# Logits out of the products that turn the state, and two additions moved from VectorE to GpSimd, in the second graph stage

## The reference

```python
x = x + _L0_gnn_ref(_layernorm(x), adj, ...)   # gated graph layer
x = x + _L0_ffn_ref(_layernorm(x), ...)        # LSTM over the nodes, then sums before and after each node
x = x + _L1_gnn_ref(_layernorm(x), adj, W, b)  # normalised graph convolution
x = x + _L1_ffn_ref(_layernorm(x), ...)        # max-plus product, hinges, gated FFN
```

```python
logits = einsum('bth,lh->btl', lstm_out, W_lin) + b_lin          # two logits a node
g = argmax(logits, axis=-1)                                      # 0 or 1 a node
w = g * lstm_out
inc = cumsum(w, axis=1); prefix = inc - w; suffix = inc[:, -1:, :] - inc
return 2.0 * lstm_out + prefix * fw_att + suffix * bw_att
```

## Time and profile before

| what | us | instructions |
|---|---|---|
| median of 3 runs (6144.3 to 6149.71) | 6147.24 | |
| the profiled execution: its own time | 6148.58 | |
| its span | 6146.8 | 107920 |
| TensorE matmul busy (PE) | 5497.9 (89%) | 31674 |
| TensorE weight load busy (PEld) | 3582.1 (58%) | 31674 |
| VectorE busy (DVE) | 4964.1 (81%) | 9353 |
| ScalarE busy (ACT) | 3352.9 (55%) | 6537 |
| GpSimd busy (POOL) | 1704.9 (28%) | 3544 |

### The profile page before, as it was taken

The page is one execution under the profiler, slowest core; times in us unless marked ns, Lnnn a source line. Parts: engine busy times, 40 slices in busy tenths (PEclk is TensorE's granted clock), DMA queues, the critical chain, the costliest instruction groups (busy, mean ns, idle before and its releaser), DMA issues. The chain is left out here.

```text
span 6146.8 us, 107920 instructions
## 1 busy us (share of the span) xinstructions
PE 5497.9 (89%) x31674; PEld 3582.1 (58%) x31674; DVE 4964.1 (81%) x9353; ACT 3352.9 (55%) x6537; POOL 1704.9 (28%) x3544
## 2 busy tenths in 40 slices
PE   9998999999899917999999994876758999999999
PEld 6666777777788815666666663543434444444444
DVE  8995444444699978999999996986858999999998
ACT  6664444444455505666666662221217878788787
POOL 3331000000254414566656662267350000000000
PEclk9999999999999969999999996997979999999999
DMA  4441000000355521222222221256352222221221
GB/s 137 136 136 54 0 0 0 0 0 0 110 177 176 174 91 62 74 72 72 73 76 72 72 72 35 86 183 234 117 190 88 68 84 82 69 84 66 88 84 48
DMA packets 359539, 528.54 MB, mean 86 GB/s; under 512 B 28000, under 2 KB 298080, under 8 KB 359424
## 3 DMA queue, kind: packets, MB, share of 16 engines
q1 hardware_dynamic: 323120, 401.16, 20.1%
q0 software_dynamic: 36304, 126.13, 6.0%
HBM read 298.06 MB, written 229.13 MB: 86 GB/s over the span
## 5 line engine op out<-in xcount | busy, mean ns | idle before, releaser
L1766 PE MATMUL t_fetched<-t_wpart,t_onehot 128*128 128x512 f32 x4096 | 1221.8, 420 | 35.9 <-DVE t_tout L1871 16.0
L1871 DVE SCALAR_TENSOR_TENSOR t_tout<-t_fetched,t_top,t_tout 128x1024 f32<-128x1024 f32 x896 | 1149.0, 1282 | 36.3 <-PE t_fetched L1766 5.1
L1766 PEld LDWEIGHTS t_fetched<-t_wpart,t_onehot 128*128 128x128 f32 x4096 | 691.7, 188 | 269.2 <-DVE t_tout L1871 131.2
L2704 DVE SCALAR_TENSOR_TENSOR f_line<-f_hinge,f_vec,f_line 128x1024 f32<-128x1024 f32 x512 | 655.0, 1279 | 79.4 <-ACT f_hinge L2582 48.0
L2194 PE MATMUL ts_fetched<-t_wpart,ts_onehot 128*128 128x512 f32 x1608 | 506.6, 449 | 166.0 <-ACT ts_onehot L2169 60.8
L604 PE MATMUL l_ps<-l_wih,l_x 128*64 128x128 f32 (+1 forms) x6144 | 544.6, 312 | 1.0 <-DVE l_ps L530 1.0
L572 ACT ACTIVATE l_act<-l_ps 128x128 f32<-128x128 f32 x1024 | 253.6, 276 | 526.0 <-PE l_ps L604 526.0
L2194 PEld LDWEIGHTS ts_fetched<-t_wpart,ts_onehot 128*128 128x128 f32 x1608 | 304.0, 207 | 317.3 <-DVE ts_tout L2262 187.4
L604 PE MATMUL l_ps<-l_whh,l_ht 128*64 128x128 f32 (+1 forms) x6144 | 488.2, 308 | 0.0
L2621 PE MATMUL f_psc<-f_x,f_wc 128*128 128x512 f32 x1024 | 483.1, 594 | 0.0
L2634 PE MATMUL f_pso<-f_fused,f_wd 128*128 128x512 f32 x1024 | 461.9, 594 | 23.1 <-DVE f_ox L2700 23.1
(11 more groups left out here) (388 smaller groups left out, 10761.9 us busy)
## 6 DMA issues: line engine op xcount, KB each, us to landing
t<-t_tout SPq DMA_DIRECT2D x128, 512.0 KB, 2.6
f_t<-t SPq DMA_DIRECT2D x64, 1024.0 KB, 5.3
g_adj<-in_adj SPq DMA_DIRECT2D x128, 256.0 KB, 3.2
g_adjt<-in_adjt SPq DMA_DIRECT2D x128, 256.0 KB, 2.8
t_x<-x_normalised SPq DMA_DIRECT2D x130, 128.0 KB, 2.4
g_x<-in_x SPq DMA_DIRECT2D x64, 256.0 KB, 2.8
x_kept<-g_x SPq DMA_DIRECT2D x64, 256.0 KB, 2.2
g_x<-x_kept SPq DMA_DIRECT2D x64, 256.0 KB, 2.8
```

The costliest lines, as they stand in the source:

```text
L1766: mm = pe.matmul(fetched[c % RING][:, h * CH:(h + 1) * CH], one_hot[g][:, c % GRP * P:(c % GRP + 1) * P], w_part[part][:, k, h * CH:(h + 1 ...
L1871: dve.scalar_tensor_tensor(t_out[j][:, :], column[:, :], value, t_out[j][:, :], ALU.add, ALU.max)\
L2704: dve.scalar_tensor_tensor(acc[:, :], source, column(u, "bend", k), acc[:, :], ALU.mult, ALU.add)\
```

## The change

TensorE no longer makes the logits by products of their own. The four transposes of `h_t` become four true products: the moving operand is `turn_lin`, for each feature half an identity of 128 columns with the two logit columns behind it, so that 130 columns come out for each node half and feature half (`ps_h` is now `[P, NT, KD, 256]`, of which 130 are used). ScalarE evacuates all of them, times 2, into `h2`. VectorE adds the two partial logits and twice the bias, which takes two additions from SBUF in place of one from PSUM, and they wait for `h2_ready`. `s` and `x2b` are computed by GpSimd: x2b behind the additions to adjt, s at the end of its body, with waits for `h2_ready` and `x2_ready`; VectorE's x2 also waits for the earlier x2b. Two constant loads are added (the identity, for each half).

```diff
--- before.py
+++ after.py
@@ -671,8 +671,8 @@
             return sems[-1]
 
         w = sb("g1_w", [P, KD, D])
-        w_lin = sb("g1_wlin", [P, KD, 2])
-        b_lin = sb("g1_blin", [P, NT, 2])
+        turn_lin = sb("g1_turnlin", [P, KD, P + 2])
+        b_lin, two_b = sb("g1_blin", [P, NT, 2]), sb("g1_twob", [P, NT, 2])
         ones_sq = sb("g1_ones_sq", [P, P])
         before = sb("g1_before", [P, P])
         after = sb("g1_after", [P, P])
@@ -687,8 +687,8 @@
         x3t_out = [sb(f"g1_x3t{j}", [P, KD, N]) for j in range(2)]
         xn3t_out = [sb(f"g1_xn3t{j}", [P, KD, N]) for j in range(2)]
         h_t = sb("g1_ht", [P, KD, N])
-        h2 = sb("g1_h2", [P, NT, D])
-        logit = sb("g1_logit", [P, NT, 2])
+        h2 = sb("g1_h2", [P, NT, KD, P + 2])
+        half_logit, logit = sb("g1_halflogit", [P, NT, 2]), sb("g1_logit", [P, NT, 2])
         picked = sb("g1_picked", [P, NT])
         whf = [sb(f"g1_whf{j}", [P, NT, D]) for j in range(2)]
         whb = [sb(f"g1_whb{j}", [P, NT, D]) for j in range(2)]
@@ -717,8 +717,7 @@
         keep = sb("g1_keep", [P, NT])
         power = sb("g1_power", [P, NT])
         dinv = [sb(f"g1_dinv{j}", [P, NT]) for j in range(2)]
-        ps_logit = ps("g1_ps_logit", [P, NT, 2])
-        ps_h = ps("g1_ps_h", [P, NT, D])
+        ps_h = ps("g1_ps_h", [P, NT, KD, 2 * P])
         ps_y = ps("g1_ps_y", [P, NT, D])
         ps_t = ps("g1_ps_t", [P, KD, N])
         ps_w = ps("g1_ps_w", [P, NT, D])
@@ -732,8 +731,8 @@
         adj_loaded = [sem(f"g1_adj_loaded{j}") for j in range(2)]
         adjt_loaded = [sem(f"g1_adjt_loaded{j}") for j in range(2)]
         x3t_stored = [sem(f"g1_x3t_stored{j}") for j in range(2)]
...
                                      "y_done"))
         s_ready, x2_ready, stats_ready, mv_ready, vare_ready, rstd_ready, x2b_ready = (
             sem("g1_" + n) for n in ("s_ready", "x2_ready", "stats_ready", "mv_ready", "vare_ready", "rstd_ready",
@@ -747,7 +746,7 @@
             sem("g1_" + n) for n in ("x3_ready", "stats3_ready", "mv3_ready", "vare3_ready", "rstd3_ready", "xn3_ready"))
         x3t_done, x3t_ready, xn3t_done, xn3t_ready = (
             sem("g1_" + n) for n in ("x3t_done", "x3t_ready", "xn3t_done", "xn3t_ready"))
-        CONST_DMAS = 11
+        CONST_DMAS = 13
         LAST = 4
 
         block = ctx.enter_context(nc.Block())
@@ -771,7 +770,9 @@
 
         @block.sync
         def _(sp):
-            sp.dma_start(w_lin[:, :, :], a["w_lin_t"].rearrange("(k p) c -> p k c", p=P)).then_inc(const_in, 16)
+            sp.dma_start(turn_lin[:, :, P:P + 2], a["w_lin_t"].rearrange("(k p) c -> p k c", p=P)).then_inc(const_in, 16)
+            for k in range(KD):
+                sp.dma_start(turn_lin[:, k, 0:P], a["ident"]).then_inc(const_in, 16)
             sp.dma_start(ident[:, :], a["ident"]).then_inc(const_in, 16)
             for t in range(NT):
                 sp.dma_start(b_lin[:, t, :], a["b_lin"].to_broadcast([P, 2])).then_inc(const_in, 16)
@@ -844,6 +845,10 @@
                         block_ = adjt_in[j][:, m, m * P:(m + 1) * P]
                         last = pool.tensor_tensor(block_, block_, ident[:, :], ALU.add)
                     last.then_inc(adjt_ready, 1)
+
+                    pool.wait_ge(x2_ready, n + 1)
+                    wait_past(pool, x3_ready, n - 1)
+                    pool.tensor_tensor(x2b[j][:, :, :], x2[:, :, :], b_all[:, :, :], ALU.add).then_inc(x2b_ready, 1)
                 if live(3):
                     n, i, j = graph(3)
 
@@ -860,6 +865,14 @@
                     pool.tensor_tensor(keep[:, :], one[:, :], is_zero[:, :], ALU.subtract).then_inc(keep_ready, 1)
                     pool.wait_ge(keep_ready, n + 1)
                     pool.tensor_tensor(dinv[j][:, :], power[:, :], keep[:, :], ALU.mult).then_inc(dinv_ready, 1)
+                if live(0):
+                    n, i, j = graph(0)
+
+                    pool.wait_ge(x1_loaded[j], 16 * i + 16)
+                    pool.wait_ge(h2_ready, n + 1)
+                    wait_past(pool, x2_ready, n - 1)
+                    pool.tensor_tensor(s[j][:, :, :].rearrange("p t (k u) -> p t k u", k=KD),
+                                       x1_in[j][:, :, :].rearrange("p t (k u) -> p t k u", k=KD), h2[:, :, :, 0:P], ALU.add).then_inc(s_ready, 1)
 
             rounds(pool, body)
 
@@ -891,7 +904,7 @@
                     act.wait_ge(h_done, n + 1)
                     wait_past(act, wh_ready, n)
                     wait_past(act, s_ready, n)
-                    act.activation(h2[:, :, :], ps_h[:, :, :], ACT.Copy, scale=2.0).then_inc(h2_ready, 1)
+                    act.activation(h2[:, :, :, :], ps_h[:, :, :, 0:P + 2], ACT.Copy, scale=2.0).then_inc(h2_ready, 1)
                 if live(-1):
                     turned_h(graph(-1)[0])
                 if live(2):
@@ -960,12 +973,11 @@
 
                     pe.wait_ge(h_t_ready, n + 1)
                     wait_past(pe, h2_ready, n)
-                    wait_past(pe, logit_ready, n)
                     for t in range(NT):
                         for k in range(KD):
-                            pe.matmul(ps_logit[:, t, :], h_t[:, k, t * P:(t + 1) * P], w_lin[:, k, :],
-                                      start=(k == 0), stop=(k == KD - 1))
-                    turn(ps_h, h_t).then_inc(h_done, 1)
+                            last = pe.matmul(ps_h[:, t, k, 0:P + 2], h_t[:, k, t * P:(t + 1) * P], turn_lin[:, k, :],
+                                             start=True, stop=True)
+                    last.then_inc(h_done, 1)
                 if live(3):
                     n, i, j = graph(3)
 
@@ -996,6 +1008,7 @@
         def _(dve):
             dve.memset(ones_sq[:, :], 1.0).then_inc(ones_set, 1)
             dve.wait_ge(const_in, 16 * CONST_DMAS)
+            dve.tensor_scalar(two_b[:, :, :], b_lin[:, :, :], 2.0, None, ALU.mult)
             dve.tensor_scalar(fw[:, :], fw[:, :], 0.5, None, ALU.mult)
             dve.tensor_scalar(bw[:, :], bw[:, :], 0.5, None, ALU.mult).then_inc(halves_ready, 1)
             dve.wait_ge(halves_ready, 1)
@@ -1024,12 +1037,11 @@
                     dve.wait_ge(y_done, n + 1)
                     dve.wait_ge(s_ready, n + 1)
                     wait_past(dve, xn_ready, n)
+                    wait_past(dve, x2b_ready, n)
                     dve.tensor_tensor(x2[:, :, :], ps_y[:, :, :], s[j][:, :, :], ALU.add).then_inc(x2_ready, 1)
                     dve.wait_ge(x2_ready, n + 1)
                     statistics(n, x2, stats, stats_ready, 0, mv, mv_ready)
 
-                    wait_past(dve, x3_ready, n - 1)
-                    dve.tensor_tensor(x2b[j][:, :, :], x2[:, :, :], b_all[:, :, :], ALU.add).then_inc(x2b_ready, 1)
                 if live(4):
                     n, i, j = graph(4)
 
@@ -1045,16 +1057,19 @@
                 if live(0):
                     n, i, j = graph(0)
 
-                    dve.wait_ge(h_done, n + 1)
-                    dve.tensor_tensor(logit[:, :, :], ps_logit[:, :, :], b_lin[:, :, :], ALU.add).then_inc(logit_ready, 1)
+                    dve.wait_ge(h2_ready, n + 1)
+                    dve.tensor_tensor(half_logit[:, :, :], h2[:, :, 0, P:P + 2], two_b[:, :, :], ALU.add)\
+                       .then_inc(half_logit_ready, 1)
+                    dve.wait_ge(half_logit_ready, n + 1)
+                    dve.tensor_tensor(logit[:, :, :], h2[:, :, 1, P:P + 2], half_logit[:, :, :], ALU.add).then_inc(logit_ready, 1)
                     dve.wait_ge(logit_ready, n + 1)
                     dve.tensor_tensor(picked[:, :], logit[:, :, 1], logit[:, :, 0], ALU.is_gt).then_inc(picked_ready, 1)
                     dve.wait_ge(picked_ready, n + 1)
-                    dve.wait_ge(h2_ready, n + 1)
                     wait_past(dve, y_done, n - 1)
                     for wh, att in ((whf, fw), (whb, bw)):
                         for t in range(NT):
-                            last = dve.scalar_tensor_tensor(wh[j][:, t, :], h2[:, t, :], picked[:, t:t + 1], att[:, :],
+                            last = dve.scalar_tensor_tensor(wh[j][:, t, :].rearrange("p (k u) -> p k u", k=KD), h2[:, t, :, 0:P],
+                                                            picked[:, t:t + 1], att[:, :].rearrange("p (k u) -> p k u", k=KD),
                                                             ALU.mult, ALU.mult)
                     last.then_inc(wh_ready, 1)
                 if live(3):
@@ -1080,12 +1095,6 @@
                     dve.wait_ge(is_zero_ready, n + 1)
                     dve.scalar_tensor_tensor(deg_safe[:, :], row_sum[:, :], 1.0, is_zero[:, :], ALU.add, ALU.add)\
                        .then_inc(deg_ready, 1)
-                if live(0):
-                    n, i, j = graph(0)
-
-                    dve.wait_ge(x1_loaded[j], 16 * i + 16)
-                    wait_past(dve, x2_ready, n - 1)
-                    dve.tensor_tensor(s[j][:, :, :], x1_in[j][:, :, :], h2[:, :, :], ALU.add).then_inc(s_ready, 1)
 
```

(4 more changed lines are left out.)

## The result

| | before | after |
|---|---|---|
| median of 4 runs each | 6147.01 us (6144.3 to 6149.71) | 6241.25 us (6239.6 to 6241.99) |
| ratio, 95% interval | | 1.0153 (1.0135 to 1.0171) |
| span of the profiled execution | 6146.8 us | 6239.9 us |

Slower by 94 us; 107 was forecast, 6254 us, with a range of 6190 to 6285.

What follows compares the result with a forecast made beforehand. A serial loop through VectorE and GpSimd was taken to bound the round, 8.88 us before. 9.47 + 1.0 + 0.15 = 10.62 us, +1.74 over 61 rounds, plus 1 us once: +107, 6254 us, range 6190 to 6285.

Steps and rivals of the forecast that it cites:

- 1: x2b leaves VectorE: its 0.58 us turn into waiting for rstd; about 0.35 us comes back in vare.
- 2: s leaves VectorE: 0.61 us less there, and rstd3 taken at 0.70 us instead of 1.16.
- 7: Uncontended loop through VectorE (5.10 us) and GpSimd (4.37): 9.47 us against 8.88, +0.59 us a round.
- the 1.5 that I named: Sign in the profile after: L1016's wait for rstd at 1.5 us or more in place of 0.26.
- 5: GpSimd's cost for each 128x512 addition: 1.27 us, bounds 0.68 to 1.83.
- 6: s stands behind dinv and ahead of the next vare in GpSimd's queue, so vare waits for all of s.
- 37 had been forecast for this case: Rival that x2b doesn't hold VectorE and only queue order counts: +37 us, 6184 us; the rival's chance 0.16.
- 8: x2b on GpSimd holds VectorE's half_logit, with two SBUF operands, and the loop: 1.0 us a round, bounds 0 to 1.27.
- 9: s on GpSimd waits for the first half of VectorE's xn3: 0.15 us a round, 0.49 if it loses to both.
- The 1 us at the start: Two more constant loads ahead of the stage's first products, 0.46 us of SyncE's queue each: 1 us, once.
- 3: Logits from h2 need one more VectorE addition: 0.19 us on the loop, bounds 0.15 to 0.3; h2 can't be late.
- 4: TensorE's eight 130-column passes take 0.88 us, 0.37 us less work a round, worth nothing off the loop.

Runs made afterwards that it cites:

- the x2b hold removed: Changed kernel with only x2b moved in GpSimd's queue, behind a wait for wh_ready: +24 us against the kernel before, ratio 1.0039.
- the second experiment: Changed kernel with the logits as before (own products, one addition from PSUM), x2b and s still on GpSimd: +75 us against the kernel before, ratio 1.0119.
- the logits alone: Changed kernel with x2b and s back on VectorE, the new logits kept: +11 us against the kernel before, ratio 1.0018.
- the three kernels with s moved: Changed kernel, x2b on VectorE, s behind wh_ready: -4.5 us against the kernel before; adjt moved there too: -10 us; also x2b behind xn3: -11 us.
- adjt alone moved: Kernel before with only GpSimd's two additions to adjt moved, behind wh_ready and ahead of vare3: 6131.03 against 6149.56 us, ratio 0.9970.
- the additions alone: Changed kernel with the old logits, x2b and s on GpSimd: +75 us against the kernel before, ratio 1.0119.

## Why the prediction was right

*The loop and not the busy shares* (steps 1, 2, 7). Right. VectorE and TensorE lost the work as worked out and the round grew. L1016's wait for rstd went from 0.26 to 0.59 and 0.87 us in alternating rounds, less than the 1.5 that I named, since xn3 itself is held by s (1.23 and 1.57 us a pair and not 0.73) and fills part of it, and in the rounds with 0.59 us 0.51 of idle time before x2 do too. TensorE was busy for 86% of the time (342.81 of 400 us) and not for 80%: that is 8.98 us a round, and I had put 8.5. Where the rest comes from stays open; it is off the path.

*The queue order of s* (5, 6). Right, with the size too large: from s's start to vare's 1.14 us, and not 1.27. With the x2b hold removed, 24 us of loss stay; 37 had been forecast for this case. With s moved out of that place, its 58 us go too.

*The hold by x2b* (8). Right: a median of 1.23 us less 0.15, so 1.08 us, taken at 1.0. By the Trainium skill ("SBUF — State Buffer", section "Who interferes with whom") half_logit would start to work when x2b ends, so end 0.15 us after it. It ended 0.02 us after it, so the trace agrees with the exclusion and with nearly the whole length: I had given the rule too little weight. The Trainium skill's distinction, in the same section, between one and two SBUF operands is what the second experiment shows (0.15 beside 1.04 us), and what moving x2b used.

*s beside VectorE* (9). Right only in every second round, and small: in the round shown s starts before xn3 and loses nothing (0.15 had been put), in the next it starts 0.09 us later behind dinv, beside xn3's first half. It is xn3 that is held, and its second half delays vare by 0.05 us.

The sum of these, in the round shown: VectorE's half (xn to vare3) 24.26 - 18.05 = 6.21 us against 6.10, the other (vare3 to xn) 18.05 - 13.79 = 4.26 against 4.52; 10.47 against 10.62. In the middle of the stage the rounds last 10.46 and 10.50 us in turn, 10.48 in the mean, and in the kernel before 8.91 and 8.95, so 8.93. The 8.88 that the forecast started from was a mean over all rounds, and the last three, in which lags fall away, are short and the same in both kernels (7.24, 8.58 and 7.05 us after, within 0.01 of those before). So the change cost 1.55 us in 60 rounds, 93 us, and not 1.74 in 61: of the 0.19 us, 0.14 lie in the loop's terms and 0.05 in that mean. The 1 us at the start can't be told in one trace.

*The logits and TensorE* (3, 4). Right: eight passes of 130 columns start 0.11 us apart, 0.89 us in all, off the path. With the logits alone a round in the middle has 9.13 us, of which TensorE is busy for 373.11 / 400, 8.52 us; before it was 398.25 / 400 of 8.93, 8.89 us. That is the 0.37 us worked out, and they bought nothing.

In the three kernels with s moved, too, VectorE waits only for rstd and before x2, and GpSimd only for VectorE (the bracket that names TensorE's ps_y before x2 in one of them stands 0.49 us behind the end of that product). So their rounds are set by the same loop, and TensorE's waits for hs follow from it. Open: how much of the gain that is missing there each of the holds takes, and what sets the round with adjt alone moved, the loop or TensorE, since both fit.

## What to carry to other kernels

When an engine's work is moved to an idle one, follow the chain through both queues: what stood in front of the short instruction that the busy engine waits for counted nearly in full here (1.14 of 1.18 us), however idle the helper was on average. Before placing a GpSimd operation, look which VectorE instructions with two SBUF operands (or tensor_scalar, such as xn and the degree's first instruction) run beside it: a four-column addition behind a 512-column one took nearly as long as the long one (1.24 and 1.33 us). It goes both ways: short instructions of GpSimd were held by VectorE's long additions. Here a single wait, which put adjt beside instructions that read at most one tile from SBUF, won 18.5 us, where moving work between the engines lost 94.

## What the runs showed that I had not expected

- GpSimd's addition for s took 1.18 us with both operands addressed in blocks of 128 columns and one strided by 130, and 1.27 us plain (in the kernel with the additions alone). Why, wasn't tested.
- With no long instruction at the end of its body, VectorE has 0.51 us of issue time (idle, with no wait that the profile shows) before x2 in every second round: in rounds 10, 12 and so on to 60, counted from 0, which are those that follow the branch back of the two-round loop. Of the other rounds from 8 to 61 only round 8 has one (0.22 us). With s there, in the kernel before and with the logits alone, none of these rounds has one.
